# A round per image instead of per tile in a two-layer shifted-window attention kernel, with fp32 scores on key partitions and value sums on query partitions

## The reference

```python
q = (xw @ Wq.T).reshape(-1, N, HEADS, d).transpose(0, 2, 1, 3)
k = (xw @ Wk.T).reshape(-1, N, HEADS, d).transpose(0, 2, 1, 3)
v = (xw @ Wv.T + bv).reshape(-1, N, HEADS, d).transpose(0, 2, 1, 3)
qn = q / jnp.maximum(jnp.linalg.norm(q, axis=-1, keepdims=True), 1e-12)
kn = k / jnp.maximum(jnp.linalg.norm(k, axis=-1, keepdims=True), 1e-12)
logits = jnp.einsum('bhnd,bhmd->bhnm', qn, kn) * scale
logits = logits + 16.0 * jax.nn.sigmoid(bias)
lg = jnp.where(mask[None, :, None], -jnp.inf, lg)
scores = jax.nn.softmax(logits, axis=-1)
o = jnp.einsum('bhnm,bhmd->bhnd', scores, v)
z = o @ Wo.T + bo
```

## Time and profile before

| what | value |
|---|---|
| runs | 1053.5, 1058.63, 1061.96 us; median 1058.63 us |
| profiled execution, span from first to last instruction | 1053.9 us |
| the profiled execution's own device time | not given apart from the span; the lowest run is 0.4 us under the span, the median 4.7 us above it |
| PE busy | 838.0 us, 80% |
| DVE busy | 965.4 us, 92% |
| ACT busy | 777.3 us, 74% |
| POOL busy | 594.2 us, 56% |

### The profile page before, as it was taken

How to read it: one execution, slowest core, us unless ns; L and a number is a source line. 1 busy time by engine, 2 the same in 40 slices (tenths; PEclk the granted TensorE clock), 3 DMA queues, 4 the chain that set the end, 5 groups by cost and what they waited for, 6 DMA issues and landing times. The chain is left out here.

```text
span 1053.9 us, 42508 instructions
## 1 busy us (share of the span) xinstructions
PE 838.0 (80%) x15130; PEld 707.3 (67%) x15130; DVE 965.4 (92%) x3558; ACT 777.3 (74%) x1743; POOL 594.2 (56%) x586
## 2 busy tenths in 40 slices
PE   2567888878888878888888887888888888888885
PEld 1456667667667767766776776777676677667764
DVE  3679899999999999999999999899999999999994
ACT  2466777777777777777777777777777777778782
POOL 4145655655565565565666565556555655656663
PEclk9989999999999999999999999999999999999998
DMA  4560000000000000000000000000000000000000
GB/s 120 152 177 6 2 3 0 0 0 0 0 0 0 0 0 0 0 0 3 2 3 2 23 23 12 20 10 20 20 20 10 20 20 10 20 20 21 13 22 33
DMA packets 14462, 21.25 MB, mean 20 GB/s; under 512 B 4489, under 2 KB 5554, under 8 KB 14386
## 3 DMA queue, kind: packets, MB, share of 16 engines
q1 hardware_dynamic: 14386, 20.24, 6.0%
HBM read 11.82 MB, written 8.42 MB: 19 GB/s over the span
## 5 line engine op out<-in xcount | busy, mean ns | idle before, releaser
L959 POOL TENSOR_TENSOR probs<-probs,exp_bias 128x512 f32<-128x512 f32 x256 | 336.6, 1335 | 187.4 <-ACT probs L619 187.4
L383 PE MATMUL bank<-w_qk,xn 128*128 128x512 f32 x768 | 219.0, 422 | 5.1 <-POOL xn L941 5.1
L950 POOL TENSOR_TENSOR q_aug<-unit,q_aug 128x256 f16<-128x256 f32 x128 | 86.3, 674 | 240.6 <-ACT k_aug L610 240.6
L491 PE MATMUL bank<-mixed,w_o 128*128 128x128 f32 x1024 | 148.7, 289 | 44.3 <-DVE mixed L848 39.0
L396 PE MATMUL bank<-w_v,xn 128*128 128x256 f32 x768 | 123.2, 297 | 72.7 <-DVE x_all L860 39.1
L566 ACT ACTIVATE v_pair<-bank 64x128 f32<-64x128 f32 x512 | 139.4, 272 | 54.7 <-PE bank L396 45.1
L491 PEld LDWEIGHTS bank<-mixed,w_o 128*128 128x128 f32 x1024 | 125.6, 193 | 60.1 <-issue 38.1
L383 PEld LDWEIGHTS bank<-w_qk,xn 128*128 128x128 f32 x768 | 140.6, 197 | 29.8 <-POOL xn L941 5.2
L396 PEld LDWEIGHTS bank<-w_v,xn 128*128 128x128 f32 x768 | 99.5, 190 | 86.1 <-issue 44.3
L540 ACT ACTIVATE q_rows<-bank 128x1024 f16<-128x1024 f16 x128 | 131.1, 1024 | 19.3 <-PE bank L412 16.7
L619 ACT ACTIVATE probs<-bank 128x512 f32<-128x512 f32 x256 | 135.9, 581 | 8.4 <-PE bank L436 8.4
(11 more groups left out here) (74 smaller groups left out, 1637.7 us busy)
## 6 DMA issues: line engine op xcount, KB each, us to landing
x_all<-in_x SPq DMA_DIRECT2D x32, 256.0 KB, 2.7
out<-x_out SPq DMA_DIRECT2D x32, 256.0 KB, 2.0
probs<-in_L_matrices SPq DMA_DIRECT2D x2, 512.0 KB
bias_rev<-table_scratch SPq DMA_DIRECT2D x32, 28.2 KB
x_out<-in_L_matrices SPq DMA_DIRECT2D x2, 256.0 KB
w_o<-in_L_matrices SPq DMA_DIRECT2D x2, 256.0 KB
consts<-const_consts SPq DMA_DIRECT2D x1, 322.0 KB
ident<-const_ident SPq DMA_DIRECT2D x1, 32.0 KB
```

Of the source, the lines that this page charges most:

```text
L383: last = nc.tensor.matmul(b_qk[e][:, :], xn[:, px, t.parity, c, e * P:(e + 1) * P], w_qk[:, pw, t.layer, c, :], start=(c == 0 and i == 0), ...
L491: last = nc.tensor.matmul(z_cols[:, c, :], w_o[:, t.layer, k, c * P:(c + 1) * P], mixed[:, e, k, :], start=(k == 0), stop=(k == CC - 1), s ...
L959: nc.gpsimd.tensor_tensor(pr, pr, exp_bias[:, t.layer, 2 * e + w, :, :], ALU.mult).then_inc(weighted, 1)
```

## The change

The rounds go from tiles to images: every step now handles both tiles of an image at once, and an iteration has one round. The pipeline is written as `now` (this job), `before`, `older`, `oldest` (one, two and three jobs back), `after` (two ahead, for the normalisation) and `ahead` (three ahead, for the moments; `WARM` = 3).

- The unit vectors stay 32-bit. The 16-bit high and low parts and their repeats are gone (L610, L871, L950), and so are the widened copies `q_rows` and `k_rows`. Queries and keys are turned as 32-bit 128 x 128 blocks (L374, 8 per image), ACT copies the queries twice into `q_own`, each time with the other head of a pair multiplied by zero (L544), DVE copies the keys once (L681).
- Scores have keys on the output partitions. A matmul has 32 contracted partitions (two heads), 64 keys and 128 columns (two heads x 64 queries), 32 of them per image (L434); four neighbours read four strips of partitions and write four banks of `ps_score`.
- Values are mixed with queries on the output partitions: the weights (`probs`) are the stationary operand, 64 x 64, and the moving one is 16 value channels beside a column of ones (`v_ones`, 17 columns), 64 matmuls per image (L455, L465). The column of ones gives the sums, so L475 and the spreading of sums (L839) are gone. `divide` (L755 to L762) reads 32 sums per partition. The result is turned back (L362, 4 transposes) and copied by ACT (`keep_mixed`, L536).
- Output projection: 4 matmuls of 256 columns per image (L383 in the new numbering), output weights re-laid by head parity.
- The sums under the roots, the steps of the refinement and the offset of the normalisation lie in PSUM, in the fourth bank of `ps_score` (`root_v`, `root_t`, `root_off`). So `score` waits for the normalisation of the image two ahead (`xn32_ready`), and `keep_variance` waits for the exponentials of the image two back. `v_cols` shares the bank of the second tile's queries and keys, so `project_v` waits for both `make_unit`. `g_cols`, `z_cols`, `back_cols` and `mix_cols` share two banks, so `mix` waits for `x_updated` and for `group_variance` of the image three ahead (`gn_step`).
- The squaring of the mean and its addition go from DVE to POOL (L841 to L844).
- Set-up: 12 instead of 7 loads per layer, 32 instead of 16 gathers of the bias table per layer, and 8 instead of 4 instructions in `mask_bias`, which now run in iterations 1 and 27.

```diff
+        ps_qk = ctx.enter_context(nc.psum_tensor("ps_qk", [P, 2, 512], F32))
+        ps_score = ctx.enter_context(nc.psum_tensor("ps_score", [P, GROUPS, 512], F32))
+        ps_mix = ctx.enter_context(nc.psum_tensor("ps_mix", [P, 2, 512], F32))
+        v_cols = ps_qk[:, 1, :].rearrange("p (e o) -> p e o", e=2)
+        root_v, root_t, root_off = ps_score[:, 3, 0:66], ps_score[:, 3, 128:194], ps_score[:, 3, 256:258]
...
+            def score(j, base, t):
...
+                if job(j, base, 2) is not None:
+                    pe.wait_ge(xn32_ready, job(j, base, 2).count(2, 2))
...
+                for e in range(2):
+                    for c in range(CC):
+                        for w in range(2):
+                            for r in range(GROUPS):
+                                at = slice(32 * r, 32 * r + 32)
+                                cols = (e * CC + c) * 2 * N
+                                last = nc.tensor.matmul(ps_score[w * N:(w + 1) * N, r, cols:cols + 2 * N], k_rows[at, e, c, w * N:(w + 1) * N],
+                                                        q_own[at, e, c, w, :, :], start=True, stop=not t.exact, skip_group_check=True)
...
+            def mix(j, base, t):
...
+                past(pe, x_updated, t.count(2, 0))
+                pe.wait_ge(v_ready, t.count(1, 1))
+                u = job(j, base, WARM)
+                if u is not None:
+                    pe.wait_ge(gn_step, u.count(3, 3))
...
+                pe.wait_ge(weighted, t.count(4, 4))
...
+                for e in range(2):
+                    for c in range(CC):
+                        for r in range(GROUPS):
+                            for a in range(2):
+                                for w in range(2):
+                                    if e + c + r + a + w == 0:
+                                        continue
+                                    at = slice(w * N, (w + 1) * N)
+                                    last = nc.tensor.matmul(mix_cols[a * N:(a + 1) * N, w, (e * CC + c) * GROUPS + r, :], probs[at, t.parity, r, e, c, a, :],
+                                                            v_ones[at, t.parity, e, c, r, a, :], start=True, stop=True, skip_group_check=True)
+                last.then_inc(mix_done, 1)
+
+            def project_v(t):
+
+                if t is None:
+                    return
+                pe.wait_ge(unit_ready, t.count(2, 2))
...
-                for e in range(2):
-                    after = job(j, base, 1) if e == 0 else None
-                    turn_q(*tile(j, base, e, 2))
-                    project_qk(*tile(j, base, e, 0))
...
+                now, before, older, oldest = (job(j, base, -k) for k in range(4))
+                project_qk(now, 0)
+                project_qk(now, 1)
+                turn_back(oldest)
+                turn(before)
+                project_out(oldest)
+                sum_groups(job(j, base, WARM))
+                score(j, base, before)
+                mix(j, base, older)
+                project_v(now)
...
+                now, before, older, oldest = (job(j, base, -k) for k in range(4))
+                square(now, 0)
+                round_xn(job(j, base, 1))
+                square(now, 1)
+                keep_mixed(oldest)
+                log_sums(j, base)
+                keep_q(before, 0)
+                seed_roots(j, base)
+                keep_q(before, 1)
+                keep_shift(before)
+                for r in range(GROUPS):
+                    exp(before, r)
+                keep_v(now)
...
+                moments(ahead)
+                sum_norms(now, 0)
+                sum_norms(now, 1)
+                keep_variance(j, base, after)
+                keep_k(before)
+                newton(j, base)
+                scale_norms(j, base, now)
+                scale_groups(j, base, after)
+                normalise(after, 0)
+                normalise(after, 1)
+                make_unit(now, 0)
+                add_residual(oldest, 0)
+                add_residual(oldest, 1)
+                make_unit(now, 1)
+                group_variance(ahead)
+                refine_shift(before)
+                cap(before)
+                divide(older)
```

More of the change, by code:

```diff
@@ L388, in project_v @@
                 if t is None:
                     return
-                if after is not None:
-                    pe.wait_ge(gn_step, after.count(GN_OPS, 1))
-                past(pe, v_ready, t.count(8, 4 * e))
-                past(pe, x_updated, t.count(2, e - 4))
-                for c in range(CC):
-                    for i, (px, pw) in enumerate(PARTS):
-                        last = nc.tensor.matmul(v_cols, xn[:, px, t.parity, c, e * P:(e + 1) * P], w_v[:, pw, t.layer, c, :],
-                                                start=(c == 0 and i == 0), stop=(c == CC - 1 and i == len(PARTS) - 1), skip_group_check=True)
@@ L548, in round_xn @@
+                past(act, norms_summed, t.count(2, e - 1))
+                nc.scalar.activation(squares[:, e, :], ps_qk[:, e, :], ACT.Square).then_inc(squared, 1)
             def round_xn(t):
@@ L581, in seed_roots, with log_sums @@
+            def log_sums(j, base):
+                t, u = job(j, base, 0), job(j, base, 2)
+                if t is None and u is None:
                     return
                 if t is not None:
-                    act.wait_ge(norms_summed, t.count(2, e + 1))
-                if after is not None:
-                    act.wait_ge(gn_step, after.count(GN_OPS, 4))
-                past(act, seeded, rooted(j, base, e))
-                nc.scalar.activation(logs[:, at], sums[:, at], ACT.Ln, bias=act_bias[:, 1:2], scale=LN_SCALE).then_inc(logged, 1)
@@ L952, in weigh @@
[L952 to L969 removed]
+                pool.wait_ge(exped, t.count(4, r + 1))
```

894 lines of the change are left out of this document (388 added, 506 removed).

## The result

The changed kernel takes 1165.38 us in the median of four runs (1161.85 to 1167.68), the kernel before on the same chip 1056.07 us (1049.0 to 1061.96). The ratio is 1.104, 95% interval 1.098 to 1.110: 10% slower. The forecast was 997 us, and the time lies outside the range too.

What follows compares the result with a forecast made beforehand. DVE was taken to bound the kernel before; after the change, the loop of waits, with PE fullest, at 14.3 us an image. 64 x 14.3 = 915 plus 80 fixed gives 995 us, median 997; range 925 to 1110 us.

Steps and rivals of the forecast that it cites:

- the rival of the clock: PE's clock falls to 1.2 GHz, three projection steps take twice their 4.6 us: about 19 us an image, 1290 us; chance 0.05.
- the sum: 64 images of 14.3 us make 915 us, plus 80 us fixed: span 995 us, median 997 us.
- the gap: PE waiting in front of `mix`, put at 0.7 to 1.4 us, with narrow matmuls in `mix` behind it.
- fixed part: Time outside the images: 72 us as before, +4 DMA issues, +5 bias products, 0 gathers, -1 deeper pipeline: 80 us.
- the loop: Waits from `project_qk` through DVE and ACT set the image: scores from 7.9, `mix` from 10.5, next image at 14.3 us.
- the main rival at 0.16: Strips of input partitions do not overlap, so scores and mixing slow: 18.1 us an image, 1238 us; partial or full loss 0.16.
- The term that each of those steps on DVE counts in full: Every microsecond of the DVE queue, `mix` and projections lengthens the image; scores are hidden up to 2.6 us.
- the work that goes: DVE loses the stalled maximum, spreading, repeats and one of two reciprocals: about 8.2 us an image against some 15.
- the mixing: 128 narrow records on PE at 14.7 ns each, 1.9 us, with two drains 2.25 us; at the highest price 8.8 us.
- 32-bit transposes: 12 transposes of 128 columns on PE taken as one record each, 1.6 us; 3.2 us if two; two-record rival 0.10.
- no stall on POOL: Refinement sums on DVE do not stall, being in PSUM; the stall rival is +3.2 us an image, chance 0.04.
- +4: Set-up: eleven more DMA issues on SP before the last weights are in, at 0.35 us each, counted as +4 us.

Runs made afterwards that it cites:

- e1: The changed kernel with six dense 128x512 matmuls, read by nothing, in PE's wait before the mixing: 1030.1 us, ratio 0.979 to the kernel before.
- e2: The changed kernel with DVE doing group variance and residual ahead of both unit vectors: 980.14 us, ratio 0.931 to the kernel before.
- e6: The changed kernel, waits kept, narrow mixing matmuls replaced by five dense ones that compute nothing of use: 1015.21 us, ratio 0.959 to the kernel before.
- e4: The changed kernel with five dense 128x512 matmuls before the scores only: 1081.71 us, ratio 1.020 to the kernel before.
- e7: e2 with ACT computing roots before the first query copy and DVE keeping variance between the sums of squares: 962.21 us, ratio 0.909 to the kernel before.
- e10: e9 with the shorter chain of e7 and DVE in the order residual, group variance, unit vectors, normalisation: 891.6 us, ratio 0.844 to the kernel before.
- e9: The changed kernel with roots, refinement and offset in SBUF instead of PSUM, scores not waiting for the normalisation: 1160.92 us, ratio 1.098 to the kernel before.
- e12: e10 with the two-column instruction ahead of the sums of squares and the normalisation in three-operand form: 861.52 us, ratio 0.818 to the kernel before.
- e3: The changed kernel with the value projection ahead of the mixing on PE: 998.66 us, ratio 0.947 to the kernel before.
- e5: The changed kernel with the DVE order of e2 and the five dense matmuls of e4 before the scores: 948.19 us, ratio 0.896 to the kernel before.

## Why the prediction was wrong

**The step that failed** is the dismissal of the rival of the clock: the sum took every step of PE at full clock, and the rival got 0.05 with the words that PE's load, 12.8 of 14.3 us, is a larger share than the 80% of now. The share over a whole image says nothing of the clock in one part of it. The prediction had the gap and the narrow matmuls in the same sentence, and then weighed them with a number that averages them away. As a size, the rival was wrong as well: it doubled the three projection steps and came to 19 us and 1290 us. In fact the query and key projection of the image shown ran at full clock (313.11 to 315.87 is 2.76 us), and what slowed was the mixing, 4.07 for 2.25 us, and the value projection, 2.62 for 1.58. That is 2.9 us an image. The mean image is 16.96 us, 2.66 above the forecast, as some images in the filling and emptying pipeline keep the clock; 64 x 2.66 = 170 us, and with a fixed part 5 us below the forecast that is the distance from the 995 us forecast for the span to the 1160 measured. e1 and e2 show that it is the clock: with the same narrow matmuls and few falls the time is 1030 and 980 us. The size agrees: the images of e6 in which the clock stays up have both waits and take 14.2 us.

**The gap was forecast too small.** The scores were priced at 1.9 us and take 1.13 (e1, 306.87 to 308.00); PE was ready for them 6.4 us into the loop and not 7.0. At full clock its load is 2.76 + 1.36 (L362 and L374) + 1.83 + 0.50 + 1.13 + 2.30 + 1.53 = 11.4 us, not 12.8. So PE idled 2.73 us in the two waits, against 0.9 + 0.7 in the sum. Faster scores made the gap longer, and filling or shortening it brings the clock back, as e1, e2 and e4 show. Overlap of input strips, whose absence was the main rival at 0.16, is there.

**Right: the loop.** From the start of the projection (313.11 - 17.08 = 296.03) the scores begin at 7.8, forecast 7.9, and `mix` at 10.4, forecast 10.5. The term that each of those steps on DVE counts in full was right, as e2, e7 and e10 show by taking them out of it. At full clock the image would be 10.4 + 2.3 + 1.55 = 14.25 us against 14.3; the full-clock images of e6 take 14.2.

**Right: the work that goes, and the mixing.** The 32-bit transposes are one record each (x8, x4), unlike the other 32-bit matmuls here, the refinement steps 0.23 us, DVE 48% busy (60% forecast of a shorter time). The mixing at full clock is 2.3 us as forecast, by the overlap of the earlier trace rows.

**Right in the result, wrong in the reason: no stall on POOL.** The prediction put it down to the operand in PSUM. But in the changed kernel the refinement and the normalisation run from 301.67 to 303.75 us, and POOL's products start only behind the scores, at 305.82 us, which themselves wait for the normalisation. The two never meet, and e9 shows the same with these operands in SBUF. Where they do meet (e10 to e12), operands in SBUF stall; the unit vectors, with one operand in PSUM, take 686 ns beside the same products, so the rule of the earlier trace rows holds. It just wasn't what decided here.

**The fixed part** was 80 us in the sum. With the mean image it is 1160 - 64 x 16.96 = 75 us. That this is near is partly luck, for its make-up was mis-sized: the first projection of queries starts at 48.34 us instead of 32.64, since DVE waits 8.75 us for the third image, whose load is issued late. Rows of the changed kernel at the start, of the DMA queue, DVE and PE:

```profile
26.37 11.20 SPq L300 DMA_DIRECT2D bias_rev<-table_scratch  x32
...
45.91 0.75 DVE L657 BATCH_NORM_STATS2 bn<-x_all 128x6 f32<-128x256 f32 x2 [8.75 <-DMA x_all<-in_x]
48.34 5.42 PE L350 MATMUL ps_qk<-w_qk,xn 128*128 128x512 f32 x12
```

That is 16 us where +4 was counted. The sum put the 32 more gathers of the bias table at 0. But the loads of the third image are issued behind the 32 gathers of the first layer, at 37.62 us; before they were issued behind 16 gathers, at 26.44. (The last image starts at 1117.12 us, and (1117.12 - 48.34) / 63 is the mean of 16.96.) The 72 us taken over from before also held what its slower images take beyond 15.35 us, one of them 20.9 (L383 from 94.11 to 115.00); a mean from first to last start counts that with the images. The rest, counted so in both, is some 26 us in the changed kernel and 28 in the kernel before, so the late start is what changed.

## What to carry to other kernels

A gap on PE is not only its own length. Where PE waits and then has narrow matmuls to do, look at the granted clock microsecond by microsecond in that part of the loop, and price the gap with the following work at 1.2 GHz. Put dense work of your own into the gap (the value projection, e3), or take what PE waits for out of the queue of the engine that makes it (e2): here the group variance was ready to be made 3 us before DVE came to it, and moving two calls turned 10% slower into 7% faster.

Before a layout is credited with avoiding a stall, check in the timeline that the two instructions run at the same time at all.

## What the runs showed of the hardware

- Work that nothing reads can save time: six matmuls of 512 columns an image took 135 us off (e1 against the changed kernel), and e5's five took 32 us off e2.
- With equal waits of 1.3 and 1.4 us the clock falls in one image of three, for 3.4 us, when matmuls of 128 x 128 with 272 columns stand behind them (e6, mean clock 0.955), and in every image, for 6.8 us, when the same place has 128 records of 17 columns, all but two of them 64 x 64 (the changed kernel, 0.81). Which property of the narrow ones matters, their partitions or their columns, wasn't tried.
- 64 records (32 matmuls) of 32 input partitions, 64 output partitions and 128 columns in 32 bits take about 1.13 us, 18 ns a record; 126 records (63 matmuls) of 64 x 64 with 17 columns 1.98 us, 15.7 ns a record at 2.4 GHz and 28 at 1.2 (3.54 us).
- A DVE instruction on two columns with a single operand in SBUF can be held for a whole POOL product (1.27 us, e10), while the reciprocal of 32 columns, also SBUF to SBUF, takes its 354 ns beside the same products. The prediction's wording, two operands in SBUF, was too narrow. The Trainium skill (SBUF — State Buffer, Who interferes with whom) names this: instructions of this form, one tensor and a constant, can enter a mode that takes the shared ports with one operand; the 1179 ns in the mean of e10 agree.
